# Another order for the drained last iteration of a four-block network

## What is computed

```python
# hawk block
alpha = jnp.exp(ALPHA_LOG_SCALE * jax.nn.softplus(forget_base) * jax.nn.sigmoid(forget))
beta = jnp.sqrt(1.0 - alpha ** 2 + 1e-06)
xs = beta * jax.nn.sigmoid(inp) * xc
h = _linear_recurrence(alpha, xs)
rglru_out = jax.nn.gelu(gate, approximate=False) * h @ W_out.T
x = x + rglru_out
xn2 = _rmsnorm(x, gamma2)
...
mlp_out = jax.nn.gelu(mgate, approximate=False) * mx @ W_shrink.T
return x + mlp_out
# mixture of experts: 8 experts, 100 places each, one shared expert matrix
probs = jax.nn.softmax(hs @ w_gate, axis=1)
best = jnp.argmax(probs, axis=1)
...
locations = jnp.cumsum(mask, axis=0) - 1
mask = mask * (locations < C).astype(jnp.int32)
...
expert_out = dispatched @ w_expert + b_expert
```

## Time and profile before

| | |
|---|---|
| median of 3 runs | 1344.32 us (1343.93 to 1347.55) |
| the profiled execution's own time | 1344.07 us |
| its span | 1342.4 us |
| busy: PE, DVE, ACT, POOL | 1200.6, 1117.4, 974.6, 806.7 us |
| drained part of the hawk and expert phase | about 1264 to 1342.4 us of the span |

### The profile page before, as it was taken

The page is one execution under the profiler, slowest core; times in us unless marked ns, Lnnn a source line. Parts: engine busy times, 40 slices in busy tenths (PEclk is TensorE's granted clock), DMA queues, the critical chain, the costliest instruction groups (busy, mean ns, idle before and its releaser), DMA issues.

```text
span 1342.4 us, 26167 instructions
## 1 busy us (share of the span) xinstructions
PE 1200.6 (89%) x8688; PEld 498.3 (37%) x8688; DVE 1117.4 (83%) x2357; ACT 974.6 (73%) x1780; POOL 806.7 (60%) x1091
## 2 busy tenths in 40 slices
PE   1789999999999999999999999988989999999863
PEld 0223233332333333333333332334645555555443
DVE  2877999999999999999999899956668878878756
ACT  1267877888788788878788777787776787787640
POOL 6304447466466566566565545366788888788752
PEclk7589999999999999999999999999999999999985
DMA  1121011011011010110110010000000000000000
GB/s 50 52 89 43 27 45 40 30 43 40 30 44 38 31 43 32 37 44 33 37 45 31 32 37 15 2 1 1 1 9 9 9 17 9 9 16 9 16 9 24
DMA packets 52517, 37.87 MB, mean 28 GB/s; under 512 B 8864, under 2 KB 51744, under 8 KB 52384
## 3 DMA queue, kind: packets, MB, share of 16 engines
q1 hardware_dynamic: 52384, 36.22, 8.4%
HBM read 6.31 MB, written 4.19 MB: 8 GB/s over the span
## 4 chain that ended last, share of the span: by engine, by line
PE 36%; DVE 25%; issue 15%; POOL 10%; ACT 10%; SPq 4%; DMA 0%; ACTq 0%; DVEq 0%; POOLq 0%
PE bank L201 10%; PE bank L182 9%; DVE neg_max L493 9%; PE bank_pair L169 4%; PE bank L228 4%; SPq L644 3%; PE bank L210 3%; ACT probs L381 2%; PE bank L235 2%; DVE probs L1178 2%; PE bank_pair L797 2%; DVE probs L1350 2%; DVE probs L1354 1%; DVE y_q L472 1%; POOL x_all L1497 1%
## 5 line engine op out<-in xcount | busy, mean ns | idle before, releaser
L381 ACT ACTIVATE probs<-bank 128x512 f32<-128x512 f32 x1024 | 569.3, 599 | 166.1 <-PE bank L182 163.8
L493 DVE TENSOR_REDUCE neg_max<-bank_pair 128x2 f32<-128x1024 f32 x512 | 610.3, 1215 | 87.4 <-PE bank_pair L169 85.5
L182 PE MATMUL bank<-q_stack,k_stack 50*128 50x512 bf16 x1024 | 353.1, 388 | 29.9 <-ACT probs L381 22.7
L201 PE MATMUL bank<-probs,v_pad 128*32 128x256 f32 x4096 | 332.2, 394 | 0.4 <-issue 0.2
L169 PE MATMUL bank_pair<-k_stack,q_stack 48*128 48x512 bf16 x1024 | 292.4, 396 | 34.0 <-DMA k_stack<-k_parts 18.1
L182 PEld LDWEIGHTS bank<-q_stack,k_stack 50*128 50x128 bf16 x1024 | 79.7, 94 | 273.8 <-ACT probs L381 233.2
L201 PEld LDWEIGHTS bank<-probs,v_pad 128*32 128x32 f32 x4096 | 83.1, 108 | 167.5 <-issue 160.3
L797 PE MATMUL bank_pair<-probs,w_gates 128*128 128x512 f32 x256 | 118.9, 609 | 1.7 <-issue 1.7
L567 POOL TENSOR_SCALAR tiny<-mv_b 128x4 f32<-128x4 f32 x16 | 3.6, 228 | 147.6 <-DVE mv_b L52 147.6
L522 POOL TENSOR_TENSOR q_rest<-q_rest,q_parts 128x512 f32<-128x512 f32 x16 | 20.2, 1261 | 119.3 <-ACT q_rest L325 119.3
L169 PEld LDWEIGHTS bank_pair<-k_stack,q_stack 48*128 48x128 bf16 x1024 | 54.1, 95 | 59.5 <-DVE neg_max L493 37.3
(11 more groups left out here) (249 smaller groups left out, 2263.6 us busy)
## 6 DMA issues: line engine op xcount, KB each, us to landing
q_stack<-q_parts SPq DMA_DIRECT2D x384, 32.0 KB
k_stack<-k_parts SPq DMA_DIRECT2D x384, 32.0 KB
x_all<-in_z_dram SPq DMA_DIRECT2D x16, 256.0 KB, 3.0
out_dram<-x_all SPq DMA_DIRECT2D x16, 256.0 KB, 2.3
q_stack<-max_rows SPq DMA_DIRECT2D x64, 8.0 KB
w_gates<-in_w_gates_dram SPq DMA_DIRECT2D x1, 512.0 KB, 3.6
w_in<-in_w_in_dram SPq DMA_DIRECT2D x1, 256.0 KB, 2.7
w_grow<-in_w_grow_dram SPq DMA_DIRECT2D x1, 256.0 KB, 3.9
```

Of the source, the lines that this page charges most:

```text
L182: nc.tensor.matmul(st_ps[h][:, :], k_stack[par][rows, p, c * P:(c + 1) * P], q_stack[par][rows, p, :], start=True, stop=True).then_inc(s[" ...
L201: mm = nc.tensor.matmul(acc[32 * g:32 * g + 32, cols], v_pad[bpar][:, kc, 4 * a + g, :], probs[:, at + g, cols], start=(t == 0 and kc == 0 ...
L381: nc.scalar.activation(probs[:, 4 * (n % RING) + g, :], st_ps[g % 2][:, :], ACT.Exp, scale=SCALE)\
L493: nc.vector.tensor_reduce(neg_max[j // 4][:, c, j % 4, :], score_ps[c % 2][:, :, :], AX_X, ALU.max, negate=True).then_inc(s["max_read"], 1)
```

## The change

The order of some steps in the drained part is written differently on four engines, and batch 14's y gets a tile and statistics of its own.

```diff
-    stats = {... for n in ("t", "x3", "y")}
+    stats = {... for n in ("t", "x3", "y", "y_odd")}
@@ TensorE, drained iteration
             forget(NB)
+            gate_in(NB)
             cumulated(NB)
-            gate_in(NB)
@@ ScalarE, drained iteration
+            decay(NB)
             route_exps(NB)
-            decay(NB)
@@ VectorE
+        def y_of(i):
+            return (acc_y, "y_odd") if i == NB + 2 else (y, "y")
...
+        def largest(i):
+            b, q = i - 4, s["top_step"]
+            wait(dve, s["logits_ps"], b + 1)
+            nc.vector.tensor_reduce(top[:, 0, :], log_ps.rearrange("p (c e) -> p c e", e=E), AX_X, ALU.max)\
+                .then_inc(q, 1)
...
+        def below_largest(i):
+            b, q = i - 4, s["top_step"]
+            wait(dve, q, 2 * b + 1)
+            wait(dve, s["route_step"], 5 * b)
+            wait(dve, s["exps_ready"], b)
+            TT(shifted[:, :, :], log_ps.rearrange("p (c e) -> p c e", e=E),
+               top[:, 0, :].unsqueeze(2).to_broadcast([P, C, E]), ALU.subtract).then_inc(q, 1)
...
+        def stats_y(i):
+            if live(i, -4):
+                aggregate(y_of(i)[1], "y", i - 4)
...
         def routed(i):
             if live(i, -4):
                 b = i - 4
+                y, which = y_of(i)
                 wait(dve, s["y_ps"], b + 1)
+                if i > NB + 2:
+                    largest(i)
+                    below_largest(i)
                 if i > NB + 1:
-                    wait(dve, s["x4_ready"], b)
+                    wait(dve, s["x4_ready"], b - 1)
                 else:
                     wait(dve, s["yc_ready"], b)
                 TT(y.rearrange("p (c d) -> p c d", c=C), bank_y[:, :].rearrange("p (c d) -> p c d", c=C),
                    consts["b_expert"][:, :].unsqueeze(1).to_broadcast([P, C, D]), ALU.add).then_inc(s["y_ready"], 1)
...
+                if i <= NB + 2:
+                    largest(i)
                 wait(dve, s["y_ready"], b + 1)
-                raw("y", "y", chunk(y))
...
+                raw(which, "y", chunk(y))
+                if i <= NB + 2:
+                    below_largest(i)
+                    stats_y(i)
@@ place_sum
+                if b < NB - 1:
+                    wait(dve, s["count_step"], 2 * b + 1)
+                    TT(counts[:, :], counts[:, :], counted[:, :], ALU.add).then_inc(s["count_step"], 1)
@@ VectorE, drained iteration
             norm_t(NB + 2)
-            routed_out(NB + 1)
             raw_x3(NB + 2)
             stats_x3(NB + 2)
             routed(NB + 2)
+            norm_x3(NB + 2)
             ranks(NB + 2)
             exps_sum(NB + 2)
             exps_inv(NB + 2)
-            norm_x3(NB + 2)
             counts_of(NB + 2)
             place(NB + 2)
+            routed_out(NB + 1)
             place_sum(NB + 2)
             routed_out(NB + 2)
             routed(NB + 3)
             ranks(NB + 3)
             exps_sum(NB + 3)
             exps_inv(NB + 3)
-            counts_of(NB + 3)
+            stats_y(NB + 3)
             place(NB + 3)
@@ GpSimd, drained iteration
             x3_sum(NB + 2)
+            root_x3(NB + 2)
             routed_root(NB + 1)
             routed_sum(NB + 1)
-            root_x3(NB + 2)
```

More of the change, by code:

```diff
@@ L708, in hawk_moe_phase @@
     xc_pad = padded[:, 0:T + TAPS - 1]
-    stats = {n: (sb(f"bn_{n}", [P, C, 6]), sb(f"mv_{n}", [P, C, 2])) for n in ("t", "x3", "y")}
+    stats = {n: (sb(f"bn_{n}", [P, C, 6]), sb(f"mv_{n}", [P, C, 2])) for n in ("t", "x3", "y", "y_odd")}
     h_sum = sb("h_sum", [P, C])
@@ L1202, in routed @@
                    consts["b_expert"][:, :].unsqueeze(1).to_broadcast([P, C, D]), ALU.add).then_inc(s["y_ready"], 1)
[L1203 to L1206, removed]
+                if i <= NB + 2:
+                    largest(i)
                 wait(dve, s["y_ready"], b + 1)
-                raw("y", "y", chunk(y))
[L1209 to L1214, removed]
+                raw(which, "y", chunk(y))
+                if i <= NB + 2:
+                    below_largest(i)
+                    stats_y(i)
         def routed_out(i):
             b = i - 4
+            y, which = y_of(i)
             wait(dve, s["rs_y_step"], 5 * (b + 1))
-            scaled(y, chunk(y), stats["y"][1], rs["y"][:, 2, :], s["yn_part"])
+            scaled(y, chunk(y), stats[which][1], rs["y"][:, 2, :], s["yn_part"])
             wait(dve, s["yn_part"], C * (i - NB))
@@ L1323, in place_sum @@
                 nc.vector.tensor_reduce(top[:, 6, :], placed[:, :, :], AX_X, ALU.add).then_inc(q, 1)
-                wait(dve, s["count_step"], 2 * b + 1)
-                TT(counts[:, :], counts[:, :], counted[:, :], ALU.add).then_inc(s["count_step"], 1)
+                if b < NB - 1:
+                    wait(dve, s["count_step"], 2 * b + 1)
+                    TT(counts[:, :], counts[:, :], counted[:, :], ALU.add).then_inc(s["count_step"], 1)
                 wait(dve, q, at + 2)
@@ L1514, in routed_root @@
                 wait_apart(gp, s["stat_y"], C * (b + 1), past_wait)
-                TT(top[:, 5, :], top[:, 4, :], stats["y"][1][:, :, 1], ALU.mult).then_inc(q, 1)
+                var = stats["y_odd" if i == NB + 2 else "y"][1][:, :, 1]
+                TT(top[:, 5, :], top[:, 4, :], var, ALU.mult).then_inc(q, 1)
                 wait_apart(gp, q, at + 2, past_wait)
```

## The result

The changed kernel takes 1338.45 us (median of 6 runs, 1335.44 to 1340.32) against 1344.89 us of the kernel before in the same 6 rounds. The ratio is 0.9948, interval 0.9935 to 0.9961: 6.4 us or 0.5% faster. The profiled execution took 1339.79 us with a span of 1338.1.

What follows compares the result with a forecast made beforehand. No engine was full; a chain of waits in the drained part was taken as the bound, at batch 15's input-gate product and behind batch 13's output. 1344.07 - 2.3 - 4.8 + 0 = 1337.0 us, range 1334.3 to 1339.6.

Steps and rivals of the forecast that it cites:

- The sum: Whole kernel: 1344.07 - 2.3 - 4.8 + 0 = 1337.0 us.
- PE and ACT: Batch 15's input-gate product directly behind forget at full clock, decay earlier on ACT: tanh moves from 1276.81 to 1272.2, by 4.6 us.
- Turn-taking: DVE's two-input steps and POOL's batch 12 work block each other, cutting the gain from 4.6 to 2.3 us.
- first half: Gate product and decay of batch 15 moved earlier on PE and ACT: worth 2.3 us, ends 4.6 and 1.8.
- The clock: PE's low clock at batch 15's transpose and wout moves along unchanged: 0 us, ends -1.2 and +2.5.
- rival 3: Clock stays low longer behind the first half or drops again up to 1307: +1.0 to +2.5 us; chance 0.18.
- rival 1: Both halves gain as summed: 1337.0 us, own range 1335.5 to 1338.5; chance 0.55.
- Second half: Near the end, batch 15's statistics and scaling go ahead of batch 13's output: worth 4.8 us.
- The arms: At the end, DVE free at 1327.25 and batch 15's y ready at 1327.2: both end together.
- Rival 5: Low clock catches PE from wout to batch 13's expert product, PE becomes bound: about +9.5, 1346.5 us; chance 0.03.

Runs made afterwards that it cites:

- e1: Kernel before with only the change's PE and ACT order (input-gate product behind forget, decay ahead of the exponential): 1342.68 us, ratio 0.9985.
- e3: Changed kernel with batch 12's sum into the residual moved on POOL to behind batch 15's residual sum: 1335.64 us, ratio 0.9926.
- e5: Changed kernel with ACT's route_exps back ahead of decay: one profiled execution, 1342.77 us; last output 63.04 us after the forget product.
- e6: Changed kernel with POOL's root_x3 of batch 15 back behind batch 13's routed_sum: last output 62.83 us after the forget product, in its profiled execution.
- e2: Changed kernel with PE and ACT order undone, leaving only the DVE and POOL part with the second y tile: 1340.47 us, ratio 0.9967.
- e4: Changed kernel with eight extra, unread PE products between batch 15's shrink product and the transpose of xn2: 1336.79 us, ratio 0.9938.
- e8: e7 with two more PE fillers, two products before batch 14's logits and four before batch 15's transpose: 1334.36 us, ratio 0.9922.
- e7: Changed kernel with e3's later batch 12 sum and e4's filler, cut to six products: 1332.69 us, ratio 0.9916.

## Why the prediction was right

The kernel became 6.4 us faster in the medians. The sum forecast 7.1; the prediction's 7.3 adds to it the 0.25 us by which one profiled execution lay under its median, which is no part of the change. In the drained part alone the profiled executions give 68.87 - 62.41 = 6.46.

- **PE and ACT.** "By 4.6 us": 4.8 (e1 has it alone, 4.8). Right. The product behind forget ran at full clock, and ACT, not PE, set the tanh.
- **Turn-taking.** "The first half is worth 2.3 us, not 4.6": 2.78 at the transpose. The mechanism is shown by e3, which takes one POOL instruction out of DVE's way and gets 2.07 of it back, and by the lengths of L1485, L1501 and the scans. The size was 0.5 too small: xs started at F + 8.45 where F + 8.7 was forecast, as the tanh gave 0.2 more, and with it the scans ended at F + 13.0, not at F + 13.4. (DVE was also not idle quite all the time before: its small steps ran until 1272.2, which changes nothing.) That `gated_in` meets L1547 is true and costs nothing by itself; what counts is L1485 against xs and the first scan.
- **The clock.** "I take this as moving along unchanged: 0." This is the term that was mis-sized. It cost 2.78 - 1.67 = 1.1 us between the transpose and the gelu, so the first half was worth 1.7. In every kernel with the earlier gate product and no filler (changed, e1, e3, e5, e6) `wout` took 3.75 or 3.76, against 3.15 before and 3.05 in e2; the growth product varied from 2.23 to 2.76. e4 shows that the low clock is the price: without it 2.0 us come back. The forecast had let the rise of the clock move along with the work, and it did not: it came 5.6 to 6.6 us after the transpose began in those five executions, 3.7 and 3.5 us after it in before and e2. From the transpose to the gelu the five took 7.1 to 7.7 us, those two 6.2 and 6.1. Why the clock rose later is open, and with one profiled execution of each kernel chance is not excluded. The reason that stood under rival 3, that PE now waits longer, is not needed for it, as e3 shows with 5.72 us of waiting. The price lies within rival 3's +1.0 to +2.5, and rival 3's sign was there: 0.50 past about 1287, which is F + 18.7, where the changed kernel has it until F + 21.0. So what happened is rival 1's two gains together with rival 3's price.
- **Second half.** "Worth 4.8 us": 4.81 in the changed kernel and 4.82 in e2. Each step came within 0.2 of its forecast in time from x3 (1317.22 in the trace before): scaling 3.13 after (forecast 3.2), batch 13's output 5.66 (5.83), last output 15.1 (15.2). `exps_inv` waited 0.24 (0.2 forecast).
- **The arms.** "Both arms end together": PE was through at 1327.65 and DVE went on at 1327.68. e8 agrees: with PE's arm 0.5 shorter the end gained 0.3.
- **Rival 5's price** does not follow from its own numbers: 30 - 19.7 is 10.3, not 9.5. Nothing else rests on it.

The sum had two errors of opposite sign, +0.5 in the turn-taking and -1.1 in the clock, and the total was out by 0.6. That it came so near is in part luck: the two gains were foreseen with their causes, the price between them was put at nothing without a reason.

## What to carry to other kernels

An engine that is shown as idle beside a moved step is not empty room: bring a two-input DVE instruction into a stretch where POOL has large work and they take turns, so that an instruction of 1.3 us can cost 2 us of chain. Look at what POOL will be doing at the new time, and move the one instruction that nobody waits for. And PE's clock does not move along with the work: here a piece of it that started at the low clock began 2.8 us earlier, the clock rose 0.5 us earlier, and 1.1 us was lost. Price such a piece at both clocks.

In an in-order queue that mixes two batches, try the last batch's chain first. Here that gave 4.8 us, more than twice the 1.7 us that the removal of a 3 us idle time gave.

## What the runs showed of the hardware

- With the same code ahead of it, F was between 1266.84 (e7) and 1272.82 (e5) in ten profiled executions. That is as much as the whole change. Single executions of these kernels can't be compared by their time; segments that start at a common event agree far better (x3 to out was 15.08 or 15.09 in six kernels), but where the clock falls or rises in the segment they can differ by up to 0.9 us (gelu to x3: 25.86 in e1, 24.96 to 24.99 in the eight without the second fall).
- The clock fell to 1.2 GHz again at batch 15's shrink product in two of ten executions (3.47 in e1, 3.45 in e5, else 2.02), with nothing different in the code there and the same 1.62 or 1.63 us of idle time ahead of it in all ten. The Trainium skill ("TensorE: Matmul & The Clock Gate", Part 1) says that the watch on the clock runs free of the kernel; these two agree with that, and no run here shows the mechanism itself.
- Extra work on PE made a kernel faster (e4): 7.0 us of products that nobody reads shortened the drained part by 2.0 us.
